# The GRU gate behind a neighbour attention: both inputs of a node turned and multiplied as one, nodes in five pieces

## The reference

```python
gat = jax.ops.segment_sum(msg, dst, num_segments=n) + bias
h = jax.nn.elu(gat)
gi = h @ W_ih.T + b_ih
gh = x @ W_hh.T + b_hh
i_r, i_z, i_n = jnp.split(gi, 3, axis=-1)
h_r, h_z, h_n = jnp.split(gh, 3, axis=-1)
r = jax.nn.sigmoid(i_r + h_r)
z = jax.nn.sigmoid(i_z + h_z)
nn_ = jnp.tanh(i_n + r * h_n)
return (1.0 - z) * nn_ + z * x
```

## Time and profile before

| what | value |
|---|---|
| runs | 4537.75, 4540.35, 4545.33 us |
| profiled execution | 4538.48 us, span 4536.9 us |
| busy share of the span | PE 67%, DVE 72%, ACT 46%, POOL 39% |
| gate, from the attention's last eviction to the end of its normalization | 3806.65 to 3893.40 us of the span |

### The profile page before, as it was taken

The page is one execution under the profiler, slowest core; times in us unless marked ns, Lnnn a source line. Parts: engine busy times, 40 slices in busy tenths (PEclk is TensorE's granted clock), DMA queues, the critical chain, the costliest instruction groups (busy, mean ns, idle before and its releaser), DMA issues. The chain is left out here.

```text
span 4536.9 us, 62983 instructions
## 1 busy us (share of the span) xinstructions
PE 3036.0 (67%) x16260; PEld 2263.2 (50%) x16261; DVE 3267.3 (72%) x7768; ACT 2103.4 (46%) x5566; POOL 1772.9 (39%) x1694
## 2 busy tenths in 40 slices
PE   5888888887355555555435555555555888779878
PEld 2444444466245545555435555555545888435534
DVE  8888888843577777777667888888858886444345
ACT  4555555551344444444344555555526886132231
POOL 0000000061577777777277777777710000021110
PEclk7999999988555555555555555555555555789988
DMA  0000000030322222222122222222240000000000
GB/s 21 0 0 0 0 0 0 0 160 1 71 66 66 66 66 66 66 66 66 32 69 65 66 66 67 67 66 66 65 166 1 1 1 2 11 4 1 4 9 8
DMA packets 136549, 183.49 MB, mean 40 GB/s; under 512 B 48763, under 2 KB 110116, under 8 KB 135396
## 3 DMA queue, kind: packets, MB, share of 16 engines
q0 software_dynamic: 50048, 77.77, 7.7%
q1 hardware_dynamic: 85348, 84.60, 6.9%
q10 hardware_dynamic: 896, 18.10, 0.9%
HBM read 158.02 MB, written 22.33 MB: 40 GB/s over the span
## 5 line engine op out<-in xcount | busy, mean ns | idle before, releaser
L1121 POOL DMA_INDIRECT adjacency<-dram_table,sorted_dst x1564 | 1597.8, 1022 | 668.8 <-issue 426.1
L1148 PE MATMUL bank<-adjacency 128*128 x3520 | 779.4, 419 | 468.9 <-ACT adjacency L1180 468.9
L1148 PEld LDWEIGHTS bank<-adjacency 128*128 128x128 f32 x3520 | 759.2, 332 | 510.7 <-issue 510.7
L1193 ACT ACTIVATE adjacency<-adjacency 128x128 f32<-128x128 bf16 x1760 | 536.8, 395 | 49.4 <-DVE adjacency L1245 49.3
L1901 PE MATMUL bank<-adjacency,cheb_parts 128*128 128x512 f16 (+1 forms) x2100 | 437.1, 367 | 52.2 <-ACTq L97 31.4
L664 ACT ACTIVATE adjacency<-bank 128x400 f32 x590 | 296.9, 503 | 318.6 <-PE bank L636 313.3
L1173 PE MATMUL bank<-ident,adjacency 128*128 128x128 f32 x440 | 117.7, 420 | 476.2 <-DVE adjacency L1302 476.2
L2170 POOL TENSOR_TENSOR cheb_y<-cheb_y,cheb_gain 128x512 f32<-128x512 f32 (+1 forms) x21 | 24.2, 1150 | 980.4 <-DVE cheb_y L2086 980.4
L1180 ACT ACTIVATE adjacency<-adjacency 128x2048 f32<-128x2048 f32 x110 | 210.3, 1912 | 408.9 <-DVE adjacency L1220 408.9
L633 PE MATMUL bank<-cell_hot,src_hot 128*128 128x400 f16 x1180 | 319.7, 353 | 74.0 <-DVE cell_hot L571 73.0
L730 POOL IOTA base_room<- 128x782 int32 x1 | 0.8, 781 | 934.9 <-ACTq L97 934.9
(11 more groups left out here) (491 smaller groups left out, 6274.4 us busy)
## 6 DMA issues: line engine op xcount, KB each, us to landing
adjacency<-dram_src_rows SPq DMA_DIRECT2D x440, 128.0 KB, 3.0
adjacency<-dram_table,sorted_dst POOLq DMA_INDIRECT x1564, 2.5
dram_adjacency<-adjacency ACTq DMA_DIRECT2D x1, 17600.0 KB, 46.3
adjacency<-dram_adjacency SPq DMA_DIRECT2D x1, 15387.5 KB, 39.4
dram_table<-adjacency SPq DMA_DIRECT2D x8, 291.0 KB, 6.2
adjacency<-dram_adjacency SPq DMA_DIRECT2D x1, 2212.5 KB, 14.5
dram_nodes<-x_nodes SPq DMA_DIRECT2D x1, 800.0 KB, 3.3
x_nodes<-dram_nodes SPq DMA_DIRECT2D x1, 800.0 KB, 5.8
```

The lines of the kernel that those rows point to most:

```text
L1121: pool.indirect_dma_start(ring[:, j % (RG * TG), :], None, dram["table"], bass.IndirectOffsetOnAxis(ap=S.dst_i[:, j:j + 1], axis=0)).then_ ...
L1148: ins = pe.matmul(sums[b % 2][:, s * W1:(s + 1) * W1], reach[:, b % 3, s, t, :], ring[:, bass.ds(at_r[s], TG), :][:, t, 0:W1], start=(t == ...
L1193: ins = act.activation(reach[:, b % 3, s, t, :], hot[:, b % 2, s, :, t], ACT.Identity, scale=-FAR, bias=score[:, b % 2, s * TG + t:s * TG ...
```

## The change

`hx` is a tile with a node's `h` in columns 0 to 63 and `x` in 64 to 127 (it shares its room with `gate`). One transpose turns both, one copy takes them to `ht` (128 rows), and one product with `w.turned` (128 rows by 256 columns, the unused quarters zero) makes all four results of a node. The biases come by a second product with two rows, `cst.ones[0:2, :]` by `w.rows`, into the same bank. Results go round six banks rather than two. The matrices and the bias are loaded before the attention; their two transposes go to bank 7. The elementwise work before and after the node loop, with the normalization's mean, centring, square and sum, is done in five pieces of five nodes, between the nodes' own steps; the subtraction of 1 moves from VectorE to ScalarE (`bend`). The root, its steps and the scaling stay as they were, over everything. A root of `eps` is added ahead of the real one.

```diff
     gat = sb("gat", [P, NB, D + 1], F32)
+    weights = gru_weights(k, sb, dram)
...
-        gru_gate(k, room(st), cst, psum, dram, x, gat)
+        gru_gate(k, room(st), cst, psum, dram, x, gat, weights)
...
+def gru_weights(k, sb, dram):
...
+        sp.dma_start(w.bias[:, :], dram["L2_gnn_bias"].unsqueeze(0).to_broadcast([P, D])).then_inc(w.loaded.sem, 16)
+        for m, name in enumerate(("ih", "hh")):
+            sp.dma_start(w.raw[:, :, m, :], dram["L2_gnn_W_" + name].rearrange("(s q) d -> q s d", s=2)).then_inc(w.loaded.sem, 16)
...
+    PIECES, EACH, R = 5, NB // 5, 6
+    ht = sb("gru_ht", [2 * D, 2, P], F32)
...
+    w.rows = sb("gru_b", [2, 4 * D], F32)
+    w.turned = sb("gru_w_t", [2 * D, 4 * D], F32)
+    eps, small = sb("gru_eps", [P, 1], F32), sb("gru_root", [P, 1], F32)
+    h, hx, part = gat[:, :, 0:D], gate, gate[:, :, 0:D]
...
+    bank = lambda i: psum[2 + i % R]
+    k.dve.memset(w.rows[:, :], 0.0)
+    cleared = k.V.mark(k.dve.memset(w.turned[:, :], 0.0))
...
+        sp.wait_ge(k.V.sem, cleared)
+        sp.wait_ge(weights.sem, weights.at(2))
+        sp.dma_start(w.rows[0:1, 0:3 * D], dram["L2_gnn_b_ih"].unsqueeze(0)).then_inc(weights.sem, 16)
+        sp.dma_start(w.rows[1:2, 0:2 * D], dram["L2_gnn_b_hh"][0:2 * D].unsqueeze(0)).then_inc(weights.sem, 16)
+        sp.dma_start(w.rows[1:2, 3 * D:4 * D], dram["L2_gnn_b_hh"][2 * D:3 * D].unsqueeze(0)).then_inc(weights.sem, 16)
...
+        for s in range(2):
+            ins = pe.transpose(psum[7][:, s * G3W // 2:(s + 1) * G3W // 2], w.raw[:, s, :, :].rearrange("q m d -> q (m d)"), cst.ident[0:G3W // 2, 0:G3W // 2])
+        ins.then_inc(w_turned.sem, 1)
...
-                pe.transpose(bank[0:D, 0:P], h[:, i, :], cst.ident[:, :])
-                pe.transpose(bank[0:D, P:2 * P], x[:, i, :], cst.ident[:, :]).then_inc(turned.sem, 1)
+                pe.transpose(psum[i % 2][:, 0:P], hx[:, i, :], cst.ident[:, :]).then_inc(turned.sem, 1)
...
-                pe.matmul(bank[:, 0:2 * D], hi, w_t[:, 0, 0:2 * D], start=True, stop=False)
-                pe.matmul(bank[:, 0:2 * D], xi, w_t[:, 1, 0:2 * D], start=False, stop=True)
-                pe.matmul(bank[:, 2 * D:G3], hi, w_t[:, 0, 2 * D:G3], start=True, stop=True)
-                pe.matmul(bank[:, G3:4 * D], xi, w_t[:, 1, 2 * D:G3], start=True, stop=True).then_inc(made.sem, 1)
+                if i >= R:
+                    pe.wait_ge(gated.sem, gated.at(i - R))
+                    pe.wait_ge(taken.sem, taken.at(i - R))
+                pe.matmul(bank(i)[:, 0:4 * D], ht[:, i % 2, :], w.turned[:, :], start=True, stop=False)
+                pe.matmul(bank(i)[:, 0:4 * D], cst.ones[0:2, :], w.rows[:, :], start=False, stop=True).then_inc(made.sem, 1)
...
+        act.activation(hx[:, :, D:2 * D], x[:, :, :], ACT.Copy).then_inc(x_laid.sem, 1)
...
+        def bend(p):
+            act.wait_ge(low_made.sem, low_made.at(p))
+            k.A(act.activation(new[:, piece(p), :], new[:, piece(p), :], ACT.Exp))
+            act.activation(new[:, piece(p), :], new[:, piece(p), :], ACT.Copy, bias=-1.0).then_inc(bent.sem, 1)
...
+        def tanh(p):
+            act.wait_ge(taken.sem, taken.at(p * EACH + EACH - 1))
+            act.activation(new[:, piece(p), :], new[:, piece(p), :], ACT.Tanh).then_inc(tanhs.sem, 1)
+
+        def square(p):
+            act.wait_ge(centred.sem, centred.at(p))
+            act.activation(new[:, piece(p), :], x[:, piece(p), :], ACT.Square).then_inc(squared.sem, 1)
+
+        for p in range(3):
+            bend(p)
+        for p in range(3, PIECES):
+            copy(2 * (p - 3))
+            copy(2 * (p - 3) + 1)
+            bend(p)
+        for i in range(NB + 1):
+            if 2 * (PIECES - 3) <= i < NB:
+                copy(i)
+            if i:
+                sigmoid(i - 1)
+            if i and i % EACH == 0:
+                tanh(i // EACH - 1)
+                if i > EACH:
+                    square(i // EACH - 2)
+        square(PIECES - 1)
+        act.activation(small[:, :], eps[:, :], ACT.Sqrt)
...
+        def low(p):
+            own = h[:, piece(p), :]
+            V(dve.tensor_tensor(own, own, wide(den, p), ALU.mult))
+            V(dve.tensor_tensor(own, own, w.bias[:, :].unsqueeze(1).to_broadcast([P, EACH, D]), ALU.add))
+            dve.tensor_scalar(new[:, piece(p), :], own, 0.0, None, ALU.min).then_inc(low_made.sem, 1)
+
+        def high(p):
+            dve.wait_ge(bent.sem, bent.at(p))
+            dve.scalar_tensor_tensor(hx[:, piece(p), 0:D], h[:, piece(p), :], 0.0, new[:, piece(p), :], ALU.max, ALU.add).then_inc(h_made.sem, 1)
+
+        def take(i):
             dve.wait_ge(gated.sem, gated.at(i))
-            V(dve.tensor_tensor(new[:, i, :], bank[:, G3:4 * D], gate[:, i, 0:D], ALU.mult))
-            dve.tensor_tensor(new[:, i, :], new[:, i, :], bank[:, 2 * D:G3], ALU.add).then_inc(taken.sem, 1)
-        dve.wait_ge(tanhs.sem, tanhs.at())
-        part = gate[:, :, 0:D]
-        V(dve.tensor_tensor(part, x[:, :, :], new[:, :, :], ALU.subtract))
-        V(dve.tensor_tensor(part, part, gate[:, :, D:2 * D], ALU.mult))
-        V(dve.tensor_tensor(part, part, new[:, :, :], ALU.add))
-        V(dve.tensor_tensor(part, part, x[:, :, :], ALU.add))
+            V(dve.tensor_tensor(new[:, i, :], bank(i)[:, 3 * D:4 * D], gate[:, i, 0:D], ALU.mult))
+            dve.tensor_tensor(new[:, i, :], new[:, i, :], bank(i)[:, 2 * D:3 * D], ALU.add).then_inc(taken.sem, 1)
+
+        def centre(p):
+            own, values, nodes = part[:, piece(p), :], new[:, piece(p), :], x[:, piece(p), :]
+            dve.wait_ge(tanhs.sem, tanhs.at(p))
+            V(dve.tensor_tensor(own, nodes, values, ALU.subtract))
+            V(dve.tensor_tensor(own, own, gate[:, piece(p), D:2 * D], ALU.mult))
+            V(dve.tensor_tensor(own, own, values, ALU.add))
+            V(dve.tensor_tensor(own, own, nodes, ALU.add))
+            V(dve.tensor_reduce(mean[:, piece(p)], own, axis=AXX, op=ALU.add))
+            V(dve.tensor_scalar(mean[:, piece(p)], mean[:, piece(p)], 1.0 / D, None, ALU.mult))
+            dve.tensor_tensor(nodes, own, wide(mean, p), ALU.subtract).then_inc(centred.sem, 1)
+
+        def spread(p):
+            dve.wait_ge(squared.sem, squared.at(p))
+            V(dve.tensor_reduce(var[:, piece(p)], new[:, piece(p), :], axis=AXX, op=ALU.add))
+
+        low(0)
+        for p in range(1, PIECES):
+            low(p)
+            high(p - 1)
+        high(PIECES - 1)
+        for p in range(PIECES + 1):
+            if p >= 1:
+                centre(p - 1)
+            if p < PIECES:
+                for i in range(p * EACH, (p + 1) * EACH):
+                    take(i)
+            if p >= 1:
+                spread(p - 1)
+        dve.tensor_scalar(var, var, 1.0 / D, EPS, ALU.mult, ALU.add).then_inc(ready.sem, 1)
...
+    rsqrt(k, var, cst.stat[:, 2, :], cst.stat[:, 3, :])
+    V(k.dve.tensor_tensor(x[:, :, :], x[:, :, :], var.unsqueeze(2).to_broadcast([P, NB, D]), ALU.mult))
...
-    layer_norm(k, gate[:, :, 0:D], x[:, :, :], new[:, :, :], cst.stat, D)
```

More of the change, by code:

```diff
@@ L1744, in gru_gate @@
     w_turned, w_made = k.sig("gru_w_turned"), k.sig("gru_w_made")
-    low_made, bent, h_made = k.sig("elu_low"), k.sig("elu_bent"), k.sig("gru_h")
+    low_made, bent, h_made, x_laid = k.sig("elu_low"), k.sig("elu_bent"), k.sig("gru_h"), k.sig("gru_ones")
     turned, copied, made = k.sig("nodes_turned"), k.sig("nodes_copied"), k.sig("nodes_made")
     gated, taken, tanhs = k.sig("gru_gated"), k.sig("gru_taken"), k.sig("gru_tanh")
-    def on_sp(sp):
[L1750 to L1753, removed]
@@ L1755, in on_pe @@
-    def on_pe(pe):
[L1756 to L1762, removed]
+    centred, squared, ready = k.sig("norm_centred"), k.sig("norm_squared"), k.sig("root_in")
+    piece = lambda p: slice(p * EACH, (p + 1) * EACH)
@@ L1782, in on_act @@
-    def on_act(act):
-        for m in range(2):
-            for s in range(2):
-                act.wait_ge(w_turned.sem, w_turned.at(2 * m + s))
-                act.activation(w_t[0:D, m, s * G3 // 2:(s + 1) * G3 // 2], psum[2 * m + s][0:D, 0:G3 // 2], ACT.Copy).then_inc(w_made.sem, 1)
-        act.wait_ge(low_made.sem, low_made.at())
-        act.activation(new[:, :, :], new[:, :, :], ACT.Exp).then_inc(bent.sem, 1)
-        for stage, i in lagged(NB, (0, 1)):
-            if stage == 0:
-                act.wait_ge(turned.sem, turned.at(i))
-                if i >= 2:
-                    act.wait_ge(made.sem, made.at(i - 2))
-                act.activation(ht[0:D, i % 2, :, :], psum[i % 2][0:D, 0:2 * P].rearrange("d (m n) -> d m n", m=2), ACT.Copy).then_inc(copied.sem, 1)
-            else:
-                act.wait_ge(made.sem, made.at(i))
-                act.activation(gate[:, i, :], psum[2 + i % 2][:, 0:2 * D], ACT.Sigmoid).then_inc(gated.sem, 1)
-        act.wait_ge(taken.sem, taken.at(NB - 1))
-        act.activation(new[:, :, :], new[:, :, :], ACT.Tanh).then_inc(tanhs.sem, 1)
@@ new lines, in on_dve @@
+    def on_dve(dve):
```

(18 more changed lines are left out.)

58 lines of the change are left out of this document (30 added, 28 removed).

## The result

The changed kernel takes 4,534.98 us (median of 20 runs, 4,526.66 to 4,539.19) against 4,545.10 for the kernel before on the same chip (20 runs, 4,537.75 to 4,548.63). The ratio is 0.9981, with a 95% interval from 0.9974 to 0.9988: some 8.6 us faster, between 5.5 and 11.8. The forecast, 18.6 us faster, is outside that interval, and the time, 4,534.98 us, is outside the range of 4,508 to 4,529.

The account below looks back on a forecast made before the run. TensorE bounds the node loop; before and after it VectorE and ScalarE wait in turns. Savings of 7.65 (entry), 1.2 (loop) and 9.7 us (tail) sum to 18.6, giving 4,521.8 us against the 4,540.35 median; range 4,508 to 4,529.

Parts of the forecast that it names:

- The entry: From the attention's last eviction to the first product: 3,814.6 against 3,822.25, 7.65 us less, bounds 6 to 9.
- The tail: From the last sigmoid to the scaling's end: 11.1 us against 20.8, so 9.7 us less.
- The main product: In the node loop, one float32 product of 256 columns over 128 rows: 0.427 us an instruction, 0.853 a product.
- few rows make nothing cheaper, so this one costs 0.853 too: In the node loop, the two-row bias product of 256 columns priced at 0.853 us, making a node 1.92 against 2.03.
- the 1.1 us put on gaps: TensorE's waits in the node loop: 0.3 us for the copy of node 4, 0.2 at each of four piece boundaries.
- Rival B: Clock rises in the new loop, VectorE's 7.4 us a piece sets the pace: 11.3 us less again, 4,510.5; chance 0.23.
- Rival C: Wide products in the loop dearer: at twice 0.427 us an instruction, loop 42.7 us more, 4,564.5; chance 0.03.
- Rival D: Squares wait for centring, holding copies and TensorE up to 3.34 us at four boundaries: 13.4 us, 4,535.2; chance 0.06.

## Why the prediction was wrong

- **The entry was right.** 7.65 us less predicted, 7.8 measured, by the mechanism named: 320-column steps at 0.48 (0.49 put), and the third piece's bend ahead of the first copy.
- **The tail was right.** 9.7 predicted, 9.89 measured; the table load of 1.28 us is waited for, as written.
- **The main product was right:** 0.42 us an instruction for 0.427.
- **The step that failed** is "few rows make nothing cheaper, so this one costs 0.853 too". Nothing was cheaper, but it was dearer: around the two-row product three steps take 0.57, 0.58 and 0.56 us in place of 0.427, and the one behind the transpose 0.27 in place of 0.213. These are the two changes between few rows and many, and the start after each, which the sum had at nothing. That is 0.48 us a node, 25 x 0.48 = 12.0 us; the 1.1 us put on gaps did not come. 49.1 + 12.0 - 1.1 = 60.0, measured 60.03.
- **How it failed:** I took the one-row product's duration, 529 ns, and set it beside a duration. The product stands alone, and the distance of its starts would not have told me either:
```profile
1120.22 0.99 PE L488 MATMUL bank<-c_row_b,ones 1*128 1x196 f32 x2 [21.40 <-DVE c_row_b L457]
```
Its two instructions start 0.99 - 0.53 = 0.46 apart, and at 0.427 / 256 a column 196 columns should start 0.33 apart. But those 0.13 us too much are what the full main product has as well behind a standstill (0.56 for 0.43). The row that has the price is one of few rows in a stream between full ones, and the trace of before has a whole stage of it, at the same granted clock of 0.50. L1534 is a transpose, L1540 a product on 64 rows:
```profile
3383.31 0.42 PE L1534 MATMUL bank<-ident,x_nodes 128*64 128x128 f32 x1
3383.66 0.69 PE L1540 MATMUL bank<-gat_w,gat_xt 64*128 64x64 f32 x2
3384.28 0.42 PE L1534 MATMUL bank<-ident,x_nodes 128*64 128x128 f32 x1
```
The steps are 0.35 into the product, 0.69 - 0.42 = 0.27 inside it and 0.35 out of it. In the loop of before, with 65 rows, the steps into and out of the products are 0.21, and 64 columns at 0.427 / 256 are 0.11. The excess is 0.14, 0.16 and 0.14, for 0.14, 0.15 and 0.13 in the changed kernel. The prediction took the row with as few rows, and not the one with the same neighbours.
- **Rival B** did not come in this kernel, and for the reason that kept it at 0.23: the two-row product. With that product padded it came at once. That its time is 4,508.1 for the 4,510.5 worked out is in part luck. Its loop is 33.7 us where B has 49.1 - 11.3 = 37.8: the clock rose 4.1 us after the first main product and not 6.4, and the first takes of two pieces are 6.69 us apart and not 7.4.
- **Rival C** had 0.03 and was nearest: an instruction dearer than 0.427 us, deciding at 0.61. The four instructions of the two products take (2.40 - 0.27) / 4 = 0.53 each. It named the width, and the rows were the cause.
- **Rival D** did not come: the last of the windows of the changed kernel above has TensorE at 57.60 of 57.60 us, over all four boundaries. Since a busy TensorE hides its pauses, the starts count more: the main products of nodes 5, 10, 15 and 20 start 2.41 us after those ahead of them, as all others do.

## What to carry to other kernels

Price an instruction by the distance between starts, never by its duration, and do so in a row that has few or many rows in its stationary operand as yours does, and stands between the same neighbours. A product that adds a bias through two rows is not free next to full products: where it stands between full products in a dense float32 loop, try it with more than 64 rows, the new ones zero. And look at the granted clock after every such edit, since here it was worth as much as the pauses.

## What the hardware showed

- At the 1.2 GHz level TensorE lost 0.13 to 0.14 us at each change between a float32 product on 2, 32 or 64 rows and one on 128, in both directions, and a further 0.15 us behind the first 256-column instruction after the change into few rows. Between 65 and 128 rows it lost nothing. In a run of eight 64-row instructions (2.4 GHz) the steps were as short as on 128 rows.
- The rows of the products decided the clock at unchanged columns and order: 65 rows kept 0.50 for 48 us, 128 rows rose to 1.00 in about 5 us. With 128-row main products, a 65-row bias product rose as well, a 64-row one did not.
- The weight loads' busy share fell from 0.98 to 0.46, half of the loads being saved. With the same five loads a node, the padded kernel had 1.45 us of loads in its 1.92 us at the lower clock, the changed one 1.10 in 2.40.
